# A graph attention layer and a linear layer on one core: the matmuls of a chunk's two row tiles take turns

## What is computed

```
e   = layernorm(x) @ a1 + (input2 @ a2).T           # 4096 x 4096
e   = where(e > 0, e, 0.2 * e)
att = softmax(where(adj > 0, e, -9e15), axis=1) * sum(adj, axis=1)
x   = x + (0.1 * att + 0.9 * adj) @ input2
x   = x + layernorm(x) @ weight.T + bias
```

## Time and profile before

| | us |
|---|---|
| median of 3 runs | 387.1 (386.89 to 387.84) |
| the profiled execution | 387.39 |
| its span | 385.5 |
| TensorE busy | 363.8 (94%) |
| VectorE busy | 311.7 (81%) |
| ScalarE busy | 246.4 (64%) |
| GpSimd busy | 134.7 (35%) |

### The profile page before, as it was taken

The page is one execution under the profiler, slowest core; times in us unless marked ns, Lnnn a source line. Parts: engine busy times, 40 slices in busy tenths (PEclk is TensorE's granted clock), DMA queues, the critical chain, the costliest instruction groups (busy, mean ns, idle before and its releaser), DMA issues.

```text
span 385.5 us, 8770 instructions
## 1 busy us (share of the span) xinstructions
PE 363.8 (94%) x3195; PEld 315.4 (82%) x3195; DVE 311.7 (81%) x791; ACT 246.4 (64%) x630; POOL 134.7 (35%) x257
## 2 busy tenths in 40 slices
PE   1599999999999999999999999999999999999991
PEld 0378888888888888888888888888888888888880
DVE  5999889989996796979687796868899696979732
ACT  4898988787670947658292855819393777767010
POOL 4588041515250606233160605325070523210111
PEclk9999999999999999999999999999999999999996
DMA  7999987566668979799998978997967710010000
GB/s 251 231 215 213 222 169 150 113 137 129 145 15 163 111 120 149 62 207 18 202 68 134 136 71 196 18 204 68 183 88 109 158 24 20 0 16 16 14 15 16
DMA packets 21769, 44.12 MB, mean 114 GB/s; under 512 B 5078, under 2 KB 13020, under 8 KB 21724
## 3 DMA queue, kind: packets, MB, share of 16 engines
q0 software_dynamic: 9216, 33.56, 60.8%
q1 hardware_dynamic: 12508, 9.98, 9.3%
HBM read 74.97 MB, written 2.11 MB: 200 GB/s over the span
## 4 chain that ended last, share of the span: by engine, by line
PE 86%; DVE 6%; ACT 5%; issue 1%; DMA 1%; SPq 0%; POOLq 0%; POOL 0%; DVEq 0%
PE acc_v L649 28%; PE acc_u L649 28%; PE acc_y L649 27%; ACT steep L487 3%; PE small L643 2%; DVE plus L959 2%; DMA plus<-in 1%; PE turned L618 1%; ACT minus L544 1%; ACT weights_v L535 1%; ACT weights_u L529 0%; DVE plus L836 0%; DVE weights_u L991 0%; DVE minus L981 0%; DVE weights_v L999 0%
## 5 line engine op out<-in xcount | busy, mean ns | idle before, releaser
L487 ACT ACTIVATE steep<-s_bc,steep_s 128x256 bf16<-128x256 f32 x512 | 208.0, 496 | 93.0 <-DMA s_bc<-s_rows 83.5
L649 PE MATMUL acc_y<-weights_y,adj_all 128*128 128x257 f16 x1024 | 122.5, 277 | 1.1 <-DVE lin L857 0.8
L649 PE MATMUL acc_u<-weights_u,plus 128*128 128x258 f16 x1024 | 120.5, 273 | 0.6 <-DVE post_st L893 0.6
L649 PE MATMUL acc_v<-weights_v,minus 128*128 128x258 f16 x1024 | 120.4, 273 | 0.0
L649 PEld LDWEIGHTS acc_y<-weights_y,adj_all 128*128 128x128 bf16 x1024 | 101.0, 99 | 17.4 <-DVE lin L857 1.1
L649 PEld LDWEIGHTS acc_u<-weights_u,plus 128*128 128x128 bf16 x1024 | 99.7, 97 | 15.5 <-DVE post_st L893 0.9
L649 PEld LDWEIGHTS acc_v<-weights_v,minus 128*128 128x128 bf16 x1024 | 99.8, 97 | 14.4
L836 DVE TENSOR_TENSOR plus<-adj_all,steep 128x2048 bf16<-128x2048 bf16 x64 | 78.3, 1224 | 10.4 <-ACT steep L487 10.4
L839 DVE TENSOR_TENSOR minus<-adj_all,plus 128x2048 bf16<-128x2048 bf16 x64 | 78.4, 1225 | 2.2
L393 POOL TENSOR_SCALAR post_var<-post_mv 128x2 f32<-128x2 f32 x15 | 3.2, 213 | 157.1 <-DVE post_mv L900 157.1
L351 POOL DMA_DIRECT2D adj_all<-adj x64 | 36.2, 584 | 6.3 <-DMA plus<-in 4.7
(11 more groups left out here) (93 smaller groups left out, 233.8 us busy)
## 6 DMA issues: line engine op xcount, KB each, us to landing
adj_all<-adj POOLq DMA_DIRECT2D x64, 512.0 KB, 14.1
x_pre<-x SPq DMA_DIRECT2D x16, 128.0 KB, 10.0
plus<-in SPq DMA_DIRECT2D x4, 512.0 KB, 5.8
x_res<-x SPq DMA_DIRECT2D x16, 128.0 KB, 11.5
out<-late SPq DMA_DIRECT2D x15, 128.0 KB, 3.7
s_bc<-s_rows SPq DMA_DIRECT2D x11, 128.0 KB, 8.4
s_rows<-pre_s SPq DMA_DIRECT2D x11, 1.0 KB
out<-late SPq DMA_DIRECT2D x2, 64.0 KB, 2.2
```

Source lines behind the costliest of these rows:

```text
L487: ins = nc.scalar.activation(steep[:, h, k, :], s1_bc[b][:, :], ACT.Relu, bias=steep_s2[:, jt:jt + 1], scale=STEEP)
L649: ins = nc.tensor.matmul(acc[:, 0:width], left[:, jt, cols(t)], right[:, jt, :, :].rearrange("p a b -> p (a b)")[:, 0:width], start=(jt == ...
```

## The change

In the opening's quarters and in slots 3 to 13 (`PAIRED`) the loop over the blocks is now the outer one: the matmul of tile 0 and that of tile 1 follow each other for each block (`pair`). A quarter thus ends for both tiles at once, and so does a product. In slots 3 to 13 TensorE does U of both, `turn`, V of both, Y of both, `linear`. U waits for both epilogues of the chunk before. ScalarE does the numerators of both tiles behind the sign tests of quarter 1 and the copies between quarters 2 and 3; VectorE does the masks of quarters 0, 1 and 2, both epilogues, and the masks of quarter 3. The first quarter of U of chunk 1 stays tile by tile, as do slots 2, 14 and 15 and the Y of chunk 3.

```diff
+PAIRED = range(3, CHUNKS - 2)
...
                     [0, 1, "first", "second", "copies", 2, 3] if c == 1 else \
+                    [0, 1, "first", "second", 2, "copies", 3] if c in PAIRED else \
                     [0, 1, "first", 2, 3, "second", "copies"] if ahead(c, 1) else \
...
+            def pair(acc, left, right, q, width=2 * WC):
+                ends = [None] * TILES
+                for jt in range(q * QJ, (q + 1) * QJ):
+                    for t in range(TILES):
+                        ends[t] = nc.tensor.matmul(acc[t][:, 0:width], left[:, jt, cols(t)],
+                                                   right[:, jt, :, :].rearrange("p a b -> p (a b)")[:, 0:width],
+                                                   start=(jt == 0), stop=(jt == JT - 1))
+                return ends
...
+            def masked_pair(acc, left, right, ready, signal, c):
+                for q in range(QUARTERS):
+                    pe.wait_ge(ready, 4 * c + q + 1)
+                    ends = pair(acc, left, right, q)
+                for ins in ends:
+                    ins.then_inc(signal, 1)
+
+            def y_pair(n, f):
+                pe.wait_ge(y_left, 2 * n)
+                for q in range(QUARTERS):
+                    pe.wait_ge(adj_landed[f][q], adj_in(n, f))
+                    ends = pair(acc_y, adj_b[f], w_y, q, WC + D)
+                for ins in ends:
+                    ins.then_inc(y_done, 1)
...
                 pe.wait_ge(adj_landed[n][q], 16)
-                for t in range(TILES):
-                    ins = quarter(acc_y[t], adj_b[n], w_y, t, q, WC + D)
-                    if q == QUARTERS - 1:
+                ends = pair(acc_y, adj_b[n], w_y, q, WC + D)
+                if q == QUARTERS - 1:
+                    for ins in ends:
                         ins.then_inc(y_done, 1)
...
-                for t in range(TILES):
-                    if n and q == 0:
+                if n and q == 0:
+                    for t in range(TILES):
                         pe.wait_ge(tile_left, t + 1)
-                    ins = quarter(acc_u[t], plus[n], w_u, t, q)
-                    if q == QUARTERS - 1:
+                        quarter(acc_u[t], plus[n], w_u, t, q)
+                else:
+                    ends = pair(acc_u, plus[n], w_u, q)
+                if q == QUARTERS - 1:
+                    for ins in ends:
                         ins.then_inc(u_done, 1)
...
-                for t in range(TILES):
-                    ins = quarter(acc_v[t], minus[n], w_v, t, q)
-                    if q == QUARTERS - 1:
+                ends = pair(acc_v, minus[n], w_v, q)
+                if q == QUARTERS - 1:
+                    for ins in ends:
                         ins.then_inc(tile_done, 1)
...
+                elif c in PAIRED:
+                    pe.wait_ge(tile_left, 2 * c)
+                    masked_pair(acc_u, plus[b], w_u, plus_ready, u_done, c)
+                    if c + 2 < SPREAD:
+                        spread(c + 2, b)
+                    turn(c - 1)
+                    masked_pair(acc_v, minus[b], w_v, minus_ready, tile_done, c)
+                    y_pair(c + 2, (f + 2) % BUFS)
+                    linear(c - 1)
+                    return
...
                 order = [0, "first", "second", 1, 2, 3] if c == 0 else \
+                    [0, 1, 2, "first", "second", 3] if c in PAIRED else \
                     [0, 1, "first", 2, 3, "second"]
```

## The result

The changed kernel takes 385.24 us (median of 8 runs, 384.45 to 385.95), the kernel before 387.04 us (8 runs, 386.74 to 387.84). The ratio is 0.9951, with a 95% interval of 0.9942 to 0.996: 1.9 us faster by the ratio and 1.8 by the medians, where no change was forecast (387.6). The profiled execution took 384.49 us at a span of 382.7, 2.8 us less than the 385.5 of before.

The account below looks back on a forecast made before the run. TensorE, with 86% of the chain of waits, nearly all in products Y, U and V, was taken as the bound. Only the opening's +0.5 us was nonzero: from the median 387.1 to 387.6 us, range 386.0 to 389.8.

Parts of the forecast that it names:

- Part 1: Rate of the 2544 moved matmuls, opening and slots: accumulator changes between -2.8 and +2.8 us, repeated operand unknown; taken as 0.
- Rival A: Paired matmuls cheaper through one moving operand: 5.5 us off, 382.1 us (376.7 at the far end); chance 0.13.
- Part 2: Opening: tile 0's later `lin` delays VectorE's masks and moves TensorE's restart from 57.90 to 58.4 us; +0.5 us.
- rival D: Opening: its delay is swallowed by a start read too late; 387.1 us, no change; chance 0.08.
- Part 3: Slots 3 to 13: both epilogues end 3.2 us before TensorE wants them, so the new order costs 0.
- rival C: Slots: s1's row landing over 4.8 us late makes TensorE wait for both epilogues; up to 397.6 us; chance 0.08.
- Part 4: Slots 14, 15 and tail: VectorE enters slot 14 0.6 us later, mostly taken up by waits for V; 0.

Follow-up runs that it names:

- e7: Kernel before, its tile-by-tile order kept, with the weight rows of Y, U and V 528 bytes apart instead of 516: 382.09 us, ratio 0.987.
- e8: Changed kernel (pairs) with the weight rows of Y, U and V 528 bytes apart: 383.76 us, ratio 0.9921 against the kernel before.
- e5: Changed kernel with pairs in the opening's quarters and slot 1 alone, slots 3 to 13 tile by tile: 387.69 us, ratio 1.0019.
- e4: Changed kernel with pairs in slots 3 to 13 alone, the opening's quarters tile by tile: 385.14 us, ratio 0.9949.
- e11: Changed kernel with Y of chunk 0 alone back to tile by tile: 385.07 us, ratio 0.9937.
- e10: Kernel before with U rows 532 bytes apart and Y reading 514-byte rows 512 bytes apart, V unchanged: 385.62 us in one run.
- e6: Kernel before, its order kept, with the weight rows of Y, U and V 520 bytes apart: 384.38 us in one run.

## Why the prediction was wrong, and where it was right

**Part 1, the rate: the step that failed.** "Of two successive matmuls with one moving operand no row tells" was right. "The nearest rows, the changes every 8 and every 32, say nothing of it goes at a change of accumulator, so the sum takes 0 here too" was not. Those rows vary how often the accumulator changes and hold fixed what matters: in all of them each matmul of a run reads the next row of weights, so they could not show what a repeated row does. They bore out the first half of part 1 (e7 and e8, at 110.0 ns each with 32 and with 1 matmul to a run) and were then used for the second. The term measured 1.0 ns for each of the 2112 matmuls in the slots, 2.14 us in all, and 0.11 us in the quarters of slot 1.

Rival A named the right place, one moving row for two matmuls, at the wrong size: 5.5 us for the whole of the 4.3 ns surplus in half of the matmuls. The surplus has two parts. 2.5 ns above columns alone are there in every layout that was run (110.0 against 107.5), and only the 1.8 above that went in any; pairs remove 1.0 of it, since the first of a pair still pays. The Trainium skill ("TensorE: Matmul & The Clock Gate", "Back-to-back issue gap") has columns / 2.4 + 2.5 ns, 110.0 for 258 columns. It gives this for an isolated matmul and says that in a stream of weight loads and matmuls it is too low at few columns and too high at many, which the prediction left out. The prediction set it aside because the trace had 111.8. The runs with separated rows, which are such streams, agree with the formula at 110.0, and what looked like a wrong figure was a cost of the layout on top of it. Against a rule, such a difference asks for its cause: it was 1.8 ns x 2544 = 4.6 us that could be had there, and e7 had 5.1 over all products.

**Part 2, the opening.** Right in the mechanism, and in the size where its premise held. VectorE in the opening of after (timeline, as the earlier trace rows):

```profile
24.14 0.29 DVE L890 SCALAR_TENSOR_TENSOR lin<-acc_y,x_res 128x128 f32<-128x128 f32 x1
...
24.73 0.28 DVE L890 SCALAR_TENSOR_TENSOR lin<-acc_y,x_res 128x128 f32<-128x128 f32 x1
...
25.32 1.22 DVE L875 TENSOR_TENSOR plus<-adj_all,steep 128x2048 bf16<-128x2048 bf16 x1
```

The two groups stand back to back, 0.59 us each, and the masks follow at once, as worked out. The chain behind them is at its limit too: 31.8 us from the masks to the restart in e5 and e4 as in before and after. The forecast of +0.49 to 0.56 at the masks is the 0.54 between e5 and e4 (11.03 and 10.63 us from the first Y to the first mask, with a Y 0.14 us shorter in e5). But the first row has no idle time before it, where the earlier trace rows has 0.47: Y ended with VectorE just done with the weights. The prediction took the execution it read for every execution. The 0.47 us of idleness was the room in which the term lived, and rival D ("swallowed") is what comes out when Y is short. The restart at 57.10 is no gain of the change: counted from the first Y it is 41.89 us, which tile by tile was reached by e7 with 41.78 and e11 with 41.93.

**Part 3, the slots: right.** VectorE in slot 8 of after, which starts at 210.94 us (as the earlier trace rows):

```profile
215.19 1.23 DVE L875 TENSOR_TENSOR plus<-adj_all,steep 128x2048 bf16<-128x2048 bf16 x1 [0.90 <-ACT steep L488]
...
222.09 1.23 DVE L875 TENSOR_TENSOR plus<-adj_all,steep 128x2048 bf16<-128x2048 bf16 x1 [1.22 <-ACT steep L488]
...
225.49 0.35 DVE L913 SCALAR_TENSOR_TENSOR num<-acc_v,ac,num 128x129 f32<-128x129 f32 x1 [0.66 <-PE acc_v L660]
...
229.56 0.29 DVE L932 BATCH_NORM_STATS2 post_st<-x 128x6 f32<-128x128 f32 x1
```

and ScalarE there (as the earlier trace rows):

```profile
211.79 6.50 ACT L488 ACTIVATE steep<-s_bc,steep_s 128x256 bf16<-128x256 f32 x16 [8.23 <-DMA s_bc<-s_rows]
```

Mask 2 starts 11.15 us into the slot (predicted: ready at 11.1) behind a wait of 1.22 (1.7), the step that wants V at 14.55 (14.6) behind 0.66 (0.7), and both epilogues end at 18.9 (18.9). TensorE waits for none of it. The row of s1 landed 0.85 us into the slot, far from the 4.8 at which rival C begins. e8 gives the limit: there the paired U of slot 3 did wait, 0.38 us. The Trainium skill ("Perfetto Trace Analysis", "Optimizing Tensor Performance") bears on that one place, where VectorE had no slack left; in the slots of after, where the epilogues end 3.0 us before the next slot (18.9 of 21.93), the trace shows no cost of both banks falling free together.

**Part 4, the tail: right.** From slot 14 to the last epilogue's wait for V both kernels need 30.48 us (342.66 to 373.14 and 345.71 to 376.19).

**The sum.** Measured terms: -2.1 for the slots, -0.1 for the quarters, +0.14 to +0.54 for the opening. That is -2.1 to -1.7 us, and the medians differ by 1.8. Taken alone, the medians of e4 (-1.85) and e5 (+0.7) would leave only -1.15; their intervals are some 0.6 us wide to either side, so this is no contradiction, but they do not confirm the sum to a tenth either.

## What to carry to other kernels

Ask of every row used as a bound what it holds fixed: it bounds only what varies in it. Where a stretch without waits is above the rate that the best layout gives, look at the operands' addresses before the order: rows of 516 bytes back to back cost this kernel 5 us, which twelve unused bytes behind each (rows 528 bytes apart) brought back without moving an instruction; four bytes (520 apart) brought back about half. Before a delay is charged in full, see how much idle time stood before the delayed step, and whether that idle time is the same in other executions.

## What the runs showed of the hardware

- A matmul whose moving row begins in the same 16 bytes in which the row of the matmul before ended takes 2.5 ns longer: 112.5 ns against 110.0 (e10's Y and U, as means). In one stream, sharing and unshared matmuls stand at 112.5 and 109.2 ns (before, e6), and where all rows lie 528 bytes apart every matmul stands at 110.0 (e7). The count of columns, 257 or 258, made no difference (Y and V of e7, 3.52 us each).
- Changes of the accumulator from one matmul to the next are free: 110.0 ns in e8 as in e7. Nor does a moving row that is read twice running save anything there.
- TensorE reached the 2.4 GHz level after 16 slow matmuls in one execution (after) and after 28 in another (before), without a pause since the first of them and in kernels whose work up to there was the same but for the order of the pairs, while the record of the granted clock read 1.00 all along. It puts the first 64 matmuls anywhere between 8.8 and 10.1 us, a spread of 1.3 us beside the 1.9 us of the change, and is to be read before two openings are compared.
